# Attention scores on four 32-row tiles of TensorE, with the mask of the exponentials on GpSimd

## The chip, the core and the metric

The kernel runs on one core of a Trainium2 chip. The metric is the device time of one execution in microseconds (us); the median of three runs is compared. The names of the engines are those of the profile: PE is TensorE (its weight loads are PEld), DVE is VectorE, ACT is ScalarE, POOL is GpSimd, SP is the queue that issues DMA transfers.

## What is computed

The whole program is two layers of a transformer. The change touches one stage of it, the causal attention of layer 0, here called stage B:

```python
b, t, e = x.shape            # 8, 512, 128
k = (x @ Wk).reshape(b, t, h, s)     # h = 16 heads of s = 8
q = (x @ Wq).reshape(b, t, h, s)
v = (x @ Wv).reshape(b, t, h, s)
k = _layernorm(k, kln_w, kln_b)
q = _layernorm(q, qln_w, qln_b)
dot = jnp.einsum('bqhs,bkhs->bhqk', q, k) * scale
causal = jnp.tril(jnp.ones((t, t), dtype=bool))
dot = jnp.where(causal, dot, -jnp.inf)
attn = jax.nn.softmax(dot, axis=-1)
out = jnp.einsum('bhqk,bkhs->bqhs', attn, v).reshape(b, t, e)
return out @ Wo + bo
```

Everything is float32 to the outside; the scores are multiplied as float32r from numbers that are split into a high and a low part.

## The kernel before, in words

Stage A makes q, k and v of all tokens, stage C runs a mixture of experts, stage B is the attention, and stages D to G are the second layer. They follow each other in the order A, C, B, D and on. In stage B a head takes `SL = 32` columns: 8 for the values' high part, 8 and 8 for the split, 2 for the row's maximum. Four heads (`G = 4`) fill 128 columns and are a *group*. A batch has four groups (`NG`), and 8 batches make 32 groups.

For a group, PE transposes the four heads' keys (item K) and queries (item Q) through bank 6, and ACT copies them to SBUF. The scores are then computed twice. The first time they stand with queries on the partitions (units `q`, `scores_q`, L1739): eight units a group, unit i is query tile i // 2 and two of the four heads, and the score matmul of (qt + 1) x 128 columns is followed by a bf16 matmul of identity and mask (L1741) that adds -1e30 above the diagonal. DVE takes the row maxima of a unit (`max_q`, L951), and after eight units writes them, negated, into the queries' spare columns (`max_rows`, L958 and L959). PE transposes the queries again (item Z). The second time the scores stand with keys on the partitions (units `k`, `scores_k`, L1753), and the maximum is already subtracted. ACT takes the exponentials (`expo`, L1429), DVE puts zeros above the diagonal (`masked`, L967), and PE multiplies with the values (`weigh_values`, L1767), in four tiles of 32 columns of the array. Then come the transposes of the outputs (item O), DVE's division by the sums (`normalise`, L973 and L978), and once a batch the transposes A, the product with Wo (item W, L1797), and DVE's residual and statistics (`residual`, L987 to L998).

A score matmul contracts over 128 partitions although a head has only 32 of them. So the keys lie in `kp`, where each head has its own 128-row copy with zeros in the other heads' rows; four DMA transfers of SP a group (`spread_keys`, L533) put them there, and POOL clears `kp` once (L645). The units share three pairs of PSUM banks in turn (`pair_of_banks`, place in the stream of q and k units modulo 3), and `free_banks` makes PE wait until the unit three places before has been read.

The order of all of this is a table of numbers, `item_times`: each item has a time in units of which a group has 8, and every engine walks through the items in the order of these times. Items that fall before `AHEAD` belong to the round before: they are issued once ahead of the loop, and then in every pass of the loop for the next pass. A pass is two batches, so there are 4 passes:

```python
for time, item in times:
    if time < ahead:
        time += length
        self.early.add(item)
```

POOL is outside of that table. It normalises the keys and the queries of one batch after another (L668 to L681), pads the values (L687) and adds the output's bias (L694), and is held back by waits alone:

```python
for n, padded, ready in ((1, ks, B_ks), (0, qs, B_qs)):
    pool.wait_ge(B_mf, B_ROUNDS.passed("misc", hb, False, "KZ"[1 - n], g_last, 0))
```

## Time and profile before

| | before |
|---|---|
| median of 3 runs (lowest to highest) | 1348.21 us (1347.28 to 1350.85) |
| the profiled execution's own time | 1348.36 us |
| its span in the trace | 1346.3 us |
| PE busy | 1055.1 us (78%) |
| DVE busy | 871.3 us (65%) |
| ACT busy | 594.5 us (44%) |
| POOL busy | 417.8 us (31%) |
| mean granted clock of PE, of full speed | 0.907 |

Busy time is the time in which an engine had an instruction of its own under way. A matmul's row begins where it begins to stream and its end is modelled, so rows of matmuls overlap, and the start of the next one says more than the end of the last. An idle time in brackets stands with what ended it. The clock has two levels, 1.2 and 2.4 GHz; 1.00 is the upper one.

### The profile page before, as it was taken

The page shows a single profiled execution, that of the slowest core. Times are in us where ns is not written, and L with a number is a line of the kernel's source. Part 1 is how long each engine was busy: PE and PEld are TensorE (multiplying, and loading weights), DVE is VectorE, ACT ScalarE, POOL GpSimd, SP SyncE. Part 2 cuts the span into 40 slices and gives each one's busy share as a digit, 9 for nine tenths or more (in the row PEclk, how much of TensorE's full clock was granted, in tenths as well). Part 3 has the DMA queues.
Part 4 walks back from the last instruction along what each step waited for, and adds up shares of the span by engine and source line. Part 5 has one row for each costly group of instructions (what it writes and reads, how often), then busy time and mean ns, then how long its engine had stood idle before and what let it go on. Part 6 is the DMA issues. An engine that isn't in the chain of part 4 may idle for free.

```text
span 1346.3 us, 22600 instructions
## 1 busy us (share of the span) xinstructions
PE 1055.1 (78%) x6332; PEld 711.3 (53%) x6332; DVE 871.3 (65%) x1881; ACT 594.5 (44%) x1109; POOL 417.8 (31%) x460
## 2 busy tenths in 40 slices
PE   7699999879898989989898778877776321499970
PEld 4355544765555656656565454444444321399960
DVE  6677741247686777778677647999996555244445
ACT  6555554125464555555465555454454101144420
POOL 4100000771412124031000023355352177266660
PEclk9899999989998999999899989899998555699995
DMA  4011113321000000000000195000001011223206
GB/s 116 32 63 62 62 62 125 128 84 25 17 25 16 19 19 23 17 17 24 18 22 19 33 156 134 1 0 0 0 0 31 6 52 34 68 79 89 96 27 186
DMA packets 64911, 66.80 MB, mean 50 GB/s; under 512 B 7842, under 2 KB 53356, under 8 KB 62800
## 3 DMA queue, kind: packets, MB, share of 16 engines
q1 hardware_dynamic: 50256, 54.52, 14.9%
q0 software_dynamic: 4608, 6.61, 1.6%
q10 hardware_dynamic: 9984, 4.80, 1.3%
q8 instruction: 43, 0.70, 0.2%
q14 instruction: 20, 0.16, 0.0%
HBM read 29.90 MB, written 29.43 MB: 44 GB/s over the span
## 4 chain that ended last, share of the span: by engine, by line
PE 40%; DVE 17%; issue 12%; ACT 3%; POOL 2%; DMA 2%; DVEq 1%; POOLq 0%; ACTq 0%; SPq 0%
PE banks L1739 6%; PE banks L1753 6%; PE banks L1767 6%; PE banks L1799 5%; PE banks L2000 5%; PE banks L1992 4%; DVE D_gun L1123 2%; PE banks L1741 2%; DVE D_dmx L1079 2%; POOL rows_dram L776 2%; DVE B_mneg L951 1%; DVE D_sc L1110 1%; DMA F_back<-y_dram 1%; PE banks L1840 1%; ACT B_ot L1435 1%
## 5 line engine op out<-in xcount | busy, mean ns | idle before, releaser
L951 DVE TENSOR_REDUCE B_mneg<-banks 128x2 f32<-128x256 f32 (+3 forms) x273 | 223.9, 822 | 110.3 <-PE banks L1741 104.0
L1429 ACT ACTIVATE B_pt<-banks 128x1024 f32<-128x1024 f32 (+3 forms) x260 | 181.6, 708 | 146.2 <-PE banks L1753 144.8
L1739 PE MATMUL banks<-B_kp,B_qt 128*128 128x128 f32 (+3 forms) x546 | 181.4, 393 | 4.2 <-DMA B_kp<-B_kt 2.3
L1753 PE MATMUL banks<-B_qt,B_kp 128*128 128x512 f32 (+3 forms) x520 | 146.3, 363 | 13.3 <-issue 7.7
L1739 PEld LDWEIGHTS banks<-B_kp,B_qt 128*128 128x128 f32 x546 | 109.4, 201 | 62.9 <-ACT B_pt L1429 43.7
L1741 PE MATMUL banks<-B_mask_q,B_identb 128*128 128x128 bf16 x546 | 125.1, 234 | 0.0
L793 POOL DMA_INDIRECT y_dram<-F_yo,F_ide x80 | 80.7, 1009 | 67.0 <-DVE F_yo L1277 42.9
L1767 PE MATMUL banks<-B_pt,B_vp 128*32 128x512 f32 (+3 forms) x1024 | 98.3, 456 | 0.0
L1505 ACT ACTIVATE D_pr<-banks,D_dmx 128x512 f32<-128x512 f32 x69 | 47.5, 688 | 106.8 <-DVE D_dmx L1079 106.8
L1563 ACT ACTIVATE F_gh<-banks 128x512 f32<-128x512 f32 (+1 forms) x96 | 50.0, 527 | 100.5 <-PE banks L1992 96.1
L967 DVE SCALAR_TENSOR_TENSOR B_pt<-B_pt,B_mask_k 128x512 f32<-128x512 f32 x129 | 93.0, 721 | 1.6 <-DVE st L998 1.0
L1753 PEld LDWEIGHTS banks<-B_qt,B_kp 128*128 128x128 f32 x520 | 81.5, 197 | 15.5 <-issue 8.3
L776 POOL DMA_INDIRECT rows_dram<-F_xs,F_rowi x64 | 63.3, 988 | 58.3 <-issue 57.7
L1741 PEld LDWEIGHTS banks<-B_mask_q,B_identb 128*128 128x128 bf16 x546 | 53.6, 98 | 44.6 <-issue 19.4
L2000 PE MATMUL banks<-F_gw,F_gh 128*128 128x128 f32 x640 | 75.3, 275 | 0.0
L1882 PE MATMUL banks<-D_qk 128*128 128x512 f32 x138 | 74.7, 635 | 0.0
L2000 PEld LDWEIGHTS banks<-F_gw,F_gh 128*128 128x128 f32 x640 | 73.9, 192 | 0.6
L1420 ACT CAST B_qt<-banks 128x512 fp32r<-128x512 f32 x68 | 39.7, 584 | 59.9 <-PE banks L1799 59.9
L1379 ACT ACTIVATE C_ec<-banks,C_nmax 128x512 f32<-128x512 f32 x68 | 47.1, 699 | 38.5 <-DVE C_nmax L894 36.9
L633 POOL CAST B_identb<-ident 128x128 bf16<-128x128 f32 x1 | 0.3, 292 | 202.2 <-ACT C_eo L1402 202.2
L1079 DVE TENSOR_REDUCE D_dmx<-banks 128x1 f32<-128x512 f32 x69 | 47.2, 684 | 13.9 <-PE banks L1882 11.9
L667 POOL MEMSET B_qs<- 128x128 f32 x8 | 1.7, 213 | 172.2 <-PE banks L1799 171.7
(275 smaller groups left out, 2240.7 us busy)
## 6 DMA issues: line engine op xcount, KB each, us to landing
B_kp<-B_kt SPq DMA_DIRECT2D x144, 64.0 KB, 2.0
comb_dram<-C_comb SPq DMA_DIRECT2D x8, 1024.0 KB, 3.8
C_cst<-comb_dram SPq DMA_DIRECT2D x8, 1024.0 KB, 4.8
rows_dram<-D_zeros SPq DMA_DIRECT2D x8, 645.0 KB, 17.1
F_xe<-rows_dram SPq DMA_DIRECT2D x8, 645.0 KB, 4.1
C_w<-w_in SPq DMA_DIRECT2D x16, 256.0 KB, 2.8
y_dram<-D_zeros SPq DMA_DIRECT2D x2, 2048.0 KB, 17.8
F_gw<-mw_in SPq DMA_DIRECT2D x16, 256.0 KB, 3.1
```

Source lines behind the costliest of these rows:

```text
L776: pool.indirect_dma_start(out=rows_dram[:, :], out_offset=bass.IndirectOffsetOnAxis(ap=rowi[:, q, k, t:t + 1], axis=0), in_=xs[:, q, k, t, ...
L793: pool.indirect_dma_start(out=y_dram[:, :], out_offset=bass.IndirectOffsetOnAxis(ap=ide[:, par, m:m + 1], axis=0), in_=yo[:, par, m, :], i ...
L951: v.tensor_reduce(mneg[:, g % 2, qt, 2 * hp:2 * hp + 2], banks2[pair_of_banks(item)][:, :, 0:(qt + 1) * P], X, ALU.max, negate=True).then_ ...
L967: v.scalar_tensor_tensor(out=w, in0=w, scalar=BIG, in1=mask_k[:].unsqueeze(1).broadcast_to([P, G, P]), op0=ALU.min, op1=ALU.mult).then_inc ...
L1079: v.tensor_reduce(dmx[:, n:n + 1], bank[2 + n % 4][:], X, ALU.max, negate=True).then_inc(D_mx, 1)
L1429: a.activation(pt[:, 2 * hp:2 * hp + 2, PT_AT[kt]:PT_AT[kt] + w], banks2[pair_of_banks(item)][:, :, 0:w], ACT.Exp).then_inc(B_ex, 1)
L1739: t_.matmul(dst, qt1[:, g % 2, qt * P:(qt + 1) * P], kp[:, g % NG, 2 * hp + h, 0:(qt + 1) * P], start=True, stop=False)
L1741: ins = t_.matmul(banks2[ring][:, h, qt * P:(qt + 1) * P], identb[:], mask_q[:], start=False, stop=True)
L1753: ins = t_.matmul(dst, kp[:, g % NG, 2 * hp + h, kt * P:(kt + 1) * P], qt2[:, g % 2, kt * P:T], start=True, stop=True)
L1767: ins = t_.matmul(bank[7][SL * r:SL * r + SL, kt * P:T], vp[:, g // NG, kt, SL * h:SL * h + SL], pt[:, r, PT_AT[kt]:PT_AT[kt] + T - kt * P ...
L1882: t_.matmul(bank[2 + n % 4][:], qk[:, b, h, t * P:(t + 1) * P], qk[:, b, 2 + h, :], start=True, stop=True).then_inc(D_sf, 1)
L2000: ins = t_.matmul(bank[4 + alt][:, t * D:(t + 1) * D], gh[:, alt, m, t * P:(t + 1) * P], gw2[:, e, m, :], start=(m == 0), stop=(m == NJ - 1))
```

## The change

- **Scores.** `kp` is gone, with its DMA transfers and its clearing. A head's score matmul reads the head's 32 rows of `kt_` and of the queries, so it runs on one of four 32-row tiles of the array, in both layouts. The units of one query (or key) tile, which hold the four heads, now stand directly behind each other in the order, and the four mask matmuls of the q layout follow behind the four score matmuls. DVE is told of the first two heads after their two masks, and of the other two after theirs.
- **Mask of the exponentials.** It leaves DVE for POOL, as an `affine_select` of 128 x 512.
- **POOL's order.** POOL now walks through the same table: the five steps of each normalisation (`nk`, `nq`), the values (`nv`) and the bias (`nb`) have times, and stand between masks. Its wait for the end of stage C (`C_os`), which stood ahead of the first bias, now stands ahead of everything in the stage.
- **Last round.** The last pass stands behind the loop, without the early items of a round that does not follow: the loop has 3 passes.

Two stretches of the instruction order show it. The first is PE in the middle of the loop, at the step in which the q units of 128 columns stand. Before, this was the second half of one q unit (the couple of L1739 and L1741 stands twice in each), and what follows:

```order
L1739 MATMUL banks<-B_kp,B_qt 128x128
L1741 MATMUL banks<-B_mask_q,B_identb 128x128
L1753 MATMUL banks<-B_qt,B_kp 128x256 x2
L1759 REGISTER_ALU
L1767 MATMUL banks<-B_pt,B_vp 32x512 x4
L1726 REGISTER_ALU
```

After, the same place of PE's order:

```order
L1746 MATMUL banks<-B_kt,B_qt 128x128 x2
L1734 REGISTER_ALU
L1746 MATMUL banks<-B_kt,B_qt 128x128 x2
L1752 MATMUL banks<-B_mask_q,B_identb 128x128 x4
L1770 REGISTER_ALU
L1778 MATMUL banks<-B_pt,B_vp 32x512 x4
L1734 REGISTER_ALU
L1764 MATMUL banks<-B_qt,B_kt 128x256 x4
L1788 REGISTER_ALU
L1810 MATMUL banks<-ident,B_qs 128x128 x4
```

One q unit, one k unit and so on alternated; now a *quarter* of a group is four score matmuls, four masks, the four products with the values, four matmuls of the other layout and four transposes. L1734 is the register that a bank wait uses, and there is one between the two halves.

The second stretch is POOL at the head of the stage. Before, the wait for the end of stage C stood behind the values of the first batch:

```order
L681 TENSOR_TENSOR B_qs<-B_n,B_qs 128x64x8 [waits pool_own]
L684 ISA [waits B_q_split]
L687 ISA [waits B_pv]
L687 COPY B_vp<-qkv 128x16x8
```

```order
L694 ISA [waits C_out_sbuf]
L694 TENSOR_TENSOR x<-x,bo 128x512
```

After, it stands ahead of the first step of the keys:

```order
L639 TENSOR_SCALAR B_lnb<-B_ln 128x128 [waits pool_own]
L668 TENSOR_TENSOR B_n<-qkv,rst 128x512 [waits C_out_sbuf,pool_own,B_constants,B_misc_full]
L672 TENSOR_TENSOR B_n<-B_n,B_lnw 128x512 [waits pool_own]
L672 TENSOR_TENSOR B_n<-B_n,B_lnb 128x512 [waits pool_own]
L680 CAST B_ks<-B_n 128x128x8 [waits pool_own]
L683 TENSOR_TENSOR B_ks<-B_n,B_ks 128x64x8 [waits pool_own]
```

The normalisation of the first batch, ten steps, moved from before that wait to behind it.

```diff
-AHEAD = 16.2
+AHEAD = 16.5
 PG = 2 * NG
 
 
 def item_times():
     for g in range(PG):
         for i in range(8):
-            yield 8 * g + i, ("q", g, i)
-            yield 8 * g + i + 12.3, ("k", g, i)
+            yield 8 * g + 2 * (i // 2) + 0.01 * (i % 2), ("q", g, i)
+            yield 8 * g + 2 * (i // 2) + 13.1 + 0.01 * (i % 2), ("k", g, i)
         for kt in range(NT):
-            yield 8 * g + 2 * kt + 14.9, ("m", g, kt)
-            yield 8 * g + 2 * kt + 16.3, ("pv", g, kt)
+            yield 8 * g + 2 * kt + 14.95, ("m", g, kt)
+            yield 8 * g + 2 * kt + 16.9, ("pv", g, kt)
         yield 8 * g - 11.2, ("K", g, 0)
         yield 8 * g - 4.8, ("Q", g, 0)
         yield 8 * g + 9.6, ("Z", g, 0)
-        yield 8 * g + 22.4 + 16.3 - 15.5, ("O", g, 0)
+        yield 8 * g + 23.9, ("O", g, 0)
         if g % NG == NG - 1:
-            yield 8 * g + 24.0, ("A", g, 0)
+            yield 8 * g + 25.0, ("A", g, 0)
             yield 8 * g + 28.0, ("W", g, 0)
+    for b in range(PG // NG):
+        for n in range(5):
+            yield 8 * NG * b - 29.3 + 1.6 * n, ("nk", b, n)
+            yield 8 * NG * b - 21.3 + 1.6 * n, ("nq", b, n)
+        yield 8 * NG * b - 13.1, ("nv", b, 0)
+        yield 8 * NG * b - 11.1, ("nb", b, 0)
...
-        kp = Bm("kp", [P, NG, G, T], F32R)
-        kt_ = Bm("kt", [P, 2, T], F32R)
+        kt_ = Bm("kt", [P, NG, T], F32R)
...
-                    for r in range(G):
-                        rows = slice(SL * r, SL * r + SL)
-                        sp.dma_start(kp[rows, g % NG, r, :].bitcast(F32), kt_[rows, g % 2, :].bitcast(F32)
-                                     ).then_inc(B_kp[g % NG], 16)
...
-            g.memset(kp[:].bitcast(F32), 0.0).then_inc(B_const, 1)
...
+            pool.wait_ge(C_os, TILES + 4)
+
+            def pool_round(it, first, last=False):
+                skips = Skip(B_ROUNDS, pool, B_md, "m") if first else None
+
+                def masked(item):
+
+                    _, g_, kt = item
+                    pool.wait_ge(B_ex, B_ROUNDS.passed("k", it, item in EARLY, "k", g_, 2 * kt + 1))
+                    pool.sem_inc(turns, 1)
+                    w = pt[:, :, PT_AT[kt]:PT_AT[kt] + P]
+                    g.affine_select(out=w, in_=w, compare_op=ALU.is_ge, fill=0.0, base=0, pattern=[[0, G], [1, P]],
+                                    channel_multiplier=-1).then_inc(B_md, 1)
...
+                for item in B_ROUNDS.order:
+                    kind, b, n = item
+                    ahead = item in EARLY
+                    if kind not in ("m", "nk", "nq", "nv", "nb") or (first and not ahead) or (last and ahead):
+                        continue
+                    if kind == "m":
+                        masked(item)
+                        if first:
+                            skips.after(item)
+                    elif kind == "nk":
+                        normed(item, 1, ks, B_ks)
+                    elif kind == "nq":
+                        normed(item, 0, qs, B_qs)
...
-                    pool.wait_ge(C_os, TILES + 4)
-                    g.tensor_tensor(xb, xb, bo[:].unsqueeze(1).broadcast_to([P, NT, D]), ALU.add).then_inc(B_bo, 1)
...
+            pool_round(-1, True)
+            with pool.Fori(0, B // 2 - 1) as it:
+                own.loop(it, 2 * 2 * 4)
+                pool_round(it, False)
+            own.end_loop(B // 2 - 1)
+            pool_round(B // 2 - 1, False, True)
...
-                def masked(item):
-
-                    _, g, kt = item
-                    dve.wait_ge(B_ex, B_ROUNDS.passed("k", it, item in EARLY, "k", g, 2 * kt + 1))
-                    w = pt[:, :, PT_AT[kt]:PT_AT[kt] + P]
-                    v.scalar_tensor_tensor(out=w, in0=w, scalar=BIG, in1=mask_k[:].unsqueeze(1).broadcast_to([P, G, P]),
-                                           op0=ALU.min, op1=ALU.mult).then_inc(B_md, 1)
...
-                        act.wait_ge(B_kp[(g - 2) % NG], 64 * B_ROUNDS.passed(f"K{(g - 2) % NG}", it, item in EARLY, "K", g - 2, 0))
+                        act.wait_ge(B_s2, B_ROUNDS.passed("k", it, item in EARLY, "k", g - NG, 7))
...
-                        pe.wait_ge(B_kp[g % NG], 64 * B_ROUNDS.passed(f"K{g % NG}", it, item in EARLY, "K", g, 0))
                     for h in range(2):
-                        dst = banks2[ring][:, h, 0:(qt + 1) * P]
-                        t_.matmul(dst, qt1[:, g % 2, qt * P:(qt + 1) * P], kp[:, g % NG, 2 * hp + h, 0:(qt + 1) * P],
-                                  start=True, stop=False)
-                        ins = t_.matmul(banks2[ring][:, h, qt * P:(qt + 1) * P], identb[:], mask_q[:],
-                                        start=False, stop=True)
-                    ins.then_inc(B_s1, 1)
+                        rows = slice(SL * (2 * hp + h), SL * (2 * hp + h) + SL)
+                        t_.matmul(banks2[ring][:, h, 0:(qt + 1) * P], qt1[rows, g % 2, qt * P:(qt + 1) * P],
+                                  kt_[rows, g % NG, 0:(qt + 1) * P], start=True, stop=False)
+                    if hp == 0:
+                        return
+                    for pair in (pair_of_banks(("q", g, i - 1)), ring):
+                        for h in range(2):
+                            ins = t_.matmul(banks2[pair][:, h, qt * P:(qt + 1) * P], identb[:], mask_q[:],
+                                            start=False, stop=True)
+                        ins.then_inc(B_s1, 1)
...
-                        dst = banks2[ring][:, h, 0:T - kt * P]
-                        ins = t_.matmul(dst, kp[:, g % NG, 2 * hp + h, kt * P:(kt + 1) * P], qt2[:, g % 2, kt * P:T],
-                                        start=True, stop=True)
+                        rows = slice(SL * (2 * hp + h), SL * (2 * hp + h) + SL)
+                        ins = t_.matmul(banks2[ring][:, h, 0:T - kt * P], kt_[rows, g % NG, kt * P:(kt + 1) * P],
+                                        qt2[rows, g % 2, kt * P:T], start=True, stop=True)
...
-            with pe.Fori(0, B // 2) as it:
+            with pe.Fori(0, B // 2 - 1) as it:
                 pe_round(it, False)
+            pe_round(B // 2 - 1, False, True)
```

## Rows read from the trace of the kernel before

Windows: the stretch and its length, busy time (and instructions) of PE, PEld, DVE, ACT and POOL, granted clock, DMA share, GB/s. Timelines: start, length, engine, line, what, count, and in brackets the idle time before it and what ended it. Forms: line and what, count | busy us, mean ns | idle before.

**Rows 1.** Windows: three groups, a plain one of them, the last of the stage.
```profile
306.83:345.23 38.40, 36.85 (x290) 23.62 (x289) 30.33 (x50) 22.48 (x36) 7.97 (x7) 1.00 0.09 22
...
332.74:345.23 12.49, 12.26 (x98) 7.87 (x97) 9.97 (x17) 7.56 (x13) 6.70 (x6) 1.00 0.09 22
...
750.98:767.00 16.02, 13.85 (x107) 8.99 (x106) 10.74 (x20) 8.45 (x14) 0.00 (x0) 1.00 0.07 17
```

**Rows 2.** Timeline of PE: values, q units, a k unit, transposes.
```profile
479.64 1.07 PE L1767 MATMUL banks<-B_pt,B_vp 128*32 128x512 f32 x8
480.64 0.33 PE L1739 MATMUL banks<-B_kp,B_qt 128*128 128x128 f32 x1
...
481.03 0.48 PE L1753 MATMUL banks<-B_qt,B_kp 128*128 128x256 f32 x2
481.35 0.60 PE L1799 MATMUL banks<-ident,B_qs 128*128 128x128 f32 x4
...
492.27 0.43 PE L1767 MATMUL banks<-B_pt,B_vp 128*32 128x128 f32 x8
492.63 0.50 PE L1739 MATMUL banks<-B_kp,B_qt 128*128 128x512 f32 x1
492.97 0.23 PE L1741 MATMUL banks<-B_mask_q,B_identb 128*128 128x128 bf16 x1
493.01 0.48 PE L1739 MATMUL banks<-B_kp,B_qt 128*128 128x512 f32 x1
```

**Rows 3.** Timeline of PE's weight loads: column tiles, then whole arrays.
```profile
738.49 0.16 PEld L1767 LDWEIGHTS banks<-B_pt,B_vp 128*32 128x32 f32 x8
...
739.84 0.31 PEld L1753 LDWEIGHTS banks<-B_qt,B_kp 128*128 128x128 f32 x2
```

**Rows 4.** Forms on DVE, 300 to 760 us.
```profile
L967 DVE SCALAR_TENSOR_TENSOR B_pt<-B_pt,B_mask_k 128x512 f32<-128x512 f32 x128 | 92.4, 722 | 1.6 <-DVE st L998 1.0 <-ACT B_pt L1429 0.5
L951 DVE TENSOR_REDUCE B_mneg<-banks 128x2 f32<-128x1024 f32 x64 | 78.1, 1221 | 6.8 <-PE banks L1741 6.3
L951 DVE TENSOR_REDUCE B_mneg<-banks 128x2 f32<-128x768 f32 x66 | 63.2, 957 | 34.3 <-PE banks L1741 33.8
L951 DVE TENSOR_REDUCE B_mneg<-banks 128x2 f32<-128x512 f32 x64 | 44.2, 691 | 36.1 <-PE banks L1741 36.1
L951 DVE TENSOR_REDUCE B_mneg<-banks 128x2 f32<-128x256 f32 x64 | 27.1, 424 | 22.1 <-PE banks L1741 16.8 <-DVE B_atok L978 5.3
```

**Rows 5.** Forms on ACT, the same stretch: the longest exponentials.
```profile
L1429 ACT ACTIVATE B_pt<-banks 128x1024 f32<-128x1024 f32 x66 | 67.7, 1026 | 42.3 <-PE banks L1753 42.1 <-ACTq L124 0.2
```

**Rows 6.** Forms on POOL, whole span: a normalisation step, a small select.
```profile
L671 POOL TENSOR_TENSOR B_n<-B_n,B_lnw 128x512 f32<-128x512 f32 x16 | 22.4, 1399 | 1.3
...
L638 POOL TENSOR_SCALAR_AFFINE_SELECT B_mask_k<-B_mask_k 128x128 f32<-128x128 f32 x1 | 0.3, 293 | 0.1
```

**Rows 7.** Timelines of POOL and of DVE near 307 us.
```profile
306.82 1.28 POOL L681 TENSOR_TENSOR B_ks<-B_n,B_ks 128x512 fp32r<-128x512 f32 x1
...
307.01 1.13 DVE L958 CAST B_qs<-B_mneg 128x16 fp32r<-128x16 f32 x1
308.17 0.19 DVE L959 TENSOR_TENSOR B_qs<-B_mneg,B_qs 128x16 fp32r<-128x16 f32 x1
```

**Rows 8.** Timeline of PE where a batch ends.
```profile
359.73 0.66 PE L1799 MATMUL banks<-ident,B_atok 128*128 128x128 f32 x4 [2.56 <-DVEq L981]
...
361.05 1.94 PE L1767 MATMUL banks<-B_pt,B_vp 128*32 128x512 f32 x8
```

**Rows 9.** Timelines of POOL and PE at the head of the stage.
```profile
265.91 1.07 POOL L668 TENSOR_TENSOR B_n<-qkv,rst 128x512 f32 x1 [0.57 <-POOL B_lnb L652]
...
277.70 1.28 POOL L681 TENSOR_TENSOR B_qs<-B_n,B_qs 128x512 fp32r<-128x512 f32 x1
...
286.68 0.45 PE L1739 MATMUL banks<-B_kp,B_qt 128*128 128x128 f32 x1 [2.29 <-DMA B_kp<-B_kt]
```

**Rows 10.** Timeline of DVE: the last addition of stage C.
```profile
281.10 0.35 DVE L940 SCALAR_TENSOR_TENSOR x<-banks,C_crs,x 128x128 f32 x1 [0.54 <-PE banks L1711]
```

More of the change, by code:

```diff
@@ L23 @@
 NEG = -1.0e30
-BIG = 3.0e38
 PT_AT = (0, T, 2 * T - P, 3 * T - 3 * P)
@@ L1001, in dve_round @@
                     kind, g, i = item
-                    if first and item not in EARLY:
+                    if (first and item not in EARLY) or (last and item in EARLY):
                         continue
@@ L1438, in act_round @@
                     kind, g, i = item
-                    if first and item not in EARLY:
+                    if (first and item not in EARLY) or (last and item in EARLY):
                         continue
@@ L1722, in free_banks @@
                 def free_banks(item):
-                    before, earlier = B_ROUNDS.place_before("unit", item, 3, first)
+                    before, earlier = B_ROUNDS.place_before("unit", item, 3, first, last)
                     if before:
@@ L1803, in pe_round @@
                     kind, g, i = item
-                    if first and item not in EARLY:
+                    if (first and item not in EARLY) or (last and item in EARLY):
                         continue
-                    if kind == "m":
+                    if kind in ("m", "nk", "nq", "nv", "nb"):
                         continue
```

135 lines of the change are left out of this document (61 added, 74 removed).

## The prediction

> **What bounds the kernel now.** I read the busy times by windows first, then the timeline of PE, then the forms on the other engines. In a plain group of stage B PE is busy for 12.26 of 12.49 us, DVE for 9.97, ACT for 7.56 and POOL for 6.70 [rows 1]: what ends a group is PE's own work. The windows are cut where a group's first product with the values begins. From the first (306.83) to the last (750.98) there are 31 groups in 444.2 us; at 12.49 each they would take 387.2, so 57 us lie in the seven places where a batch ends. One of them shows what they are [rows 8]: the transposes A wait 2.56 us for DVE, and right behind that the values block takes 1.94 us where it took 1.07 elsewhere [rows 2]; PE was idle, and the block ran at the lower clock. So three things can be won: PE's work per group, the ends of batches, and the early items in the last pass.
>
> **PE's work per group.** I price blocks by the distance between starts. Four tiles side by side are in the trace already, by columns: the values block takes 1.00 us at 512 columns and 0.36 at 128 [rows 2], which is 0.15 fixed and 0.21 for each 128 columns. A score matmul is cheaper per column: in a row with its mask (0.04 us, 492.97 to 493.01) it takes 0.38 at 512, and two with their masks take 0.39 at 128 [rows 2], so 0.34 and 0.155 alone, or 0.06 for each 128 columns more. Four row tiles side by side are then 0.15 + 0.06 n, or 0.21, 0.27, 0.33, 0.39 us for n = 1 to 4. That is the cheap end. The dear end is no overlap: four scores in a row, 0.62, 0.87, 1.11, 1.36. Between them, with matmuls side by side and weight loads in a row, three loads at 0.12 (two take 0.31, one some 0.19) come on top: 0.57, 0.63, 0.69, 0.75. Eight loads of the column tiles take 0.16 us together [rows 3], 0.007 apart, so loads of different tiles do overlap; those are of 32 columns, ours of 128. I take 0.25, 0.30, 0.36, 0.41, near the cheap end. Four masks in a row: 0.04 each if their loads are covered and 0.10 each if not, and the array changes its form before and behind them; I take 0.30 a block. Four transposes take 0.43 with the change (they stand as 0.60 long, 0.17 of which is the tail) [rows 2].
>
> The changes of form can be seen only as part of the fixed 0.15 of the values block. The Trainium skill says (TensorEngine Tiling (Array Packing), Key Properties) that switching the tiling mode drains TensorE. A quarter now has five changes where it had two to three, so the trace's fixed part agrees with that, and by the rule alone nothing could be won at the 128-column forms.
>
> A quarter of a group on PE is then q block + masks + values (1.00, 0.78, 0.57, 0.36) + k block (256, 128, 512, 384 columns) + transposes: 2.3, 2.1, 2.1, 1.9, in all 8.3 us against 12.3. (Four k matmuls of 256 columns cost 0.64 now [rows 2], 0.30 then.)
>
> **But PE is no longer the bound.** The banks are three pairs, taken in turn. In the new order a quarter uses four units: q-a, q-b, k-a, k-b. By the modulo, q-a waits until DVE has read the q-b before it, and DVE cannot start until both q units and their first two masks are through. So PE and DVE take turns in a quarter: 0.05 us for the signal, the q block, 0.06 for the second mask, 0.26 for the last matmul's way and the signal, and two reductions. The reductions are 0.424, 0.691, 0.957 and 1.221 us [rows 4]. With the blocks above: 0.62 + 0.85 = 1.47; 0.67 + 1.38 = 2.05; 0.73 + 1.91 = 2.64; 0.78 + 2.44 = 3.22. The mask that leaves DVE (0.722 us, four a group [rows 4]) gives DVE 2.9 us a group, which this turn-taking uses up.
>
> In the first quarter DVE also has the row maxima and `normalise`, 1.3 us with their waits. These read SBUF, and POOL is in their way: the cast that takes 0.2 us elsewhere took 1.13 beside a POOL instruction that ended at 308.10, and its neighbour behind it 0.19 [rows 7]. POOL's work per group grows from 3.9 us (15.7 for a batch, ten steps like the 1.4 us of [rows 6] among it) by four masks. A select of 128 columns took 0.29 us; for 512 that is at most four times as much, 1.17, and 0.6 if most of the 0.29 is fixed. So POOL is busy for 60 to 80% of a group, and I add 1.0 us for the four short instructions. First quarter: 2.3 + 0.85 = 3.1, above PE's 2.3. Second: PE, 2.1. Third: 2.64 and 0.1 for a bank that waits on the exponentials (1.03 us each [rows 5]). Fourth: 3.22 + 0.2 for the same. Sum **11.35 us** for 12.49. Cheap end, without POOL in the way and with the cheap blocks: 10.3. Dear end, loads in a row: 3.15 + 2.8 + 3.0 + 3.6 = 12.55, and up to 13.
>
> The Trainium skill says (SBUF — State Buffer, The single rule) that VectorE and GpSimd share one pair of ports by an exclusive lock. Row and rule agree for the casts; by the rule the reductions, which read PSUM, stay untouched.
>
> The masks themselves hide. The longest case is the 512-column k block of the third quarter: its exponentials end about 4.0 us after that quarter's start, its mask 5.4 us (0.2 for the signals), and the values ask for it behind two quarters and a q block, 2.75 + 3.4 + 0.65 = 6.8 us. The cover is 1.4 us, which is one normalisation step that POOL may be in when the mask comes due; beyond it each us late is a us of PE. The transfers into `kp` are costed at nothing: SP has nothing else to issue, and only the first of them ended a wait [rows 9].
>
> **The sum, against the profiled execution's 1348.36 us** (span 1346.3; the median, 1348.21, is the same):
> - 29 plain steps (31 less two in the tail) x (12.49 - 11.35) = -33. Cheap end -64, dear end +15.
> - Ends of batches, 57 us: A stood 0.8 places behind O and stands 1.1 behind now, with a values block of 1.0 us between, so most of 2.56 us and of the lower clock behind it go; W's residual and statistics on DVE come on top where DVE now bounds. 57 becomes 42: -15, ends -25 and 0.
> - The last pass: its early q and k items go. In the last 16.02 us PE worked for 13.85 [rows 1], and in the group before as much. Two groups (12.5 + 16.0) become one chain of exponentials (six quarters' worth, some 7.6 us and two copies) and the same end: -12, ends -14 and -8.
> - The head: POOL's ten steps took from 265.91 to 278.98 [rows 9], ahead of stage C's end at 281.45 [rows 10]. They start there now: 281.65 + 13.1 = 294.8, the transposes at the lower clock 1.2, the copy 0.7: the first scores at 296.8 instead of 286.68. +10, ends +9 and +11. The transfers that ended the wait there (2.29 us [rows 9]) and the clearing of `kp` go, but neither is last any more.
>
> In all -50: **1298 us**.
>
> **The rivals.**
> - *The row tiles do not run side by side* (the other side). Blocks of 0.62 to 1.36 lengthen each turn: quarters of 3.15, 3.0, 3.5, 4.2, a group of 13.8, +39, with the other terms (-15, -8, +10) about 1374. For it: no row of this trace has 32-row tiles. Against: the column tiles overlap [rows 2, 3]. It decides from a group of 13.1 us, blocks some 0.43 us longer on average than mine.
> - *The turn-taking costs all of PE's gain*: POOL in the way more often, loads half in a row, a group of 12.5. What is left is -15 - 12 + 10: 1331.
> - *The lower clock.* PE idles 1 to 1.5 us in the last quarters. One idle time of 2.56 us brought the lower clock [rows 8]; if every second group falls to it for a quarter (+1.5 us), +22: 1320.
> - *Late masks.* A select over 2.4 us makes POOL the bound, 3.9 + 4 x 2.4 = 13.5 us a group, +29: 1360. The 0.29 us row speaks against it.
> - *Better than that*: cheap blocks, POOL seldom in the way, a group of 10.3: 1262 to 1267.
>
> **How the numbers follow.** My forecast 0.50 (1275 to 1320), the better case 0.12, the turn-taking 0.14, the clock 0.08, no overlap 0.12, late masks 0.04. The range leaves out part of the better case and the two slow ones: 1258 to 1352. About 0.3% (4 us) is what a measurement of this kernel tells from no change. Faster: 0.50 + 0.12 + 0.13 + 0.07 = 0.82; same 0.04; slower 0.14.
>
> **What would show it.** The distance of a group's first values blocks: 11.35 us, with DVE the last to end a wait of q units and PE idle for 2 to 3 us a group. Four scores of 512 columns less than 0.5 us from first start to the first mask. The select on POOL between 0.6 and 1.2 us, and L958 and L959 over 0.5 us on average. The first score near 297 us. No wait over 1 us ahead of A. The forecast is wrong if a group takes over 12.5 or under 10.3 us; if the four scores start 0.12 us or more apart it was the loads.

## The result, and the profile after

| | before | changed |
|---|---|---|
| median of four runs (lowest to highest) | 1349.53 us (1347.28 to 1353.77) | 1397.47 us (1390.08 to 1400.99) |
| ratio, 95% interval | | 1.034 [1.029, 1.039] |
| span of the profiled execution | 1346.3 us | 1399.1 us |
| start of the first group's values block | 306.83 | 323.40 |
| from there to the last group's: 31 steps | 444.2 us | 481.6 us |
| behind that block | 595.3 us | 594.1 us |

The kernel is 3.4% slower. Of the 52.8 us that its span grew by, 16.6 lie ahead of the first values block and 37.4 in the 31 steps behind it, which I call the **stage time** from here on. The page of the changed kernel, busy times and granted clock by slices:

```profile
PE 1078.8 (77%) x6224; PEld 655.8 (47%) x6224; DVE 762.6 (55%) x1731; ACT 580.4 (41%) x1097; POOL 483.1 (35%) x585
...
PEclk9899999966687768655858879999999655599995
```

Stage B fills the ninth to the twenty-fourth digit, and they are 5 to 8 where before they were 8 or 9, twelve of the sixteen 9. By windows (columns as in [rows 1]): the stage, a group with a high clock, one with a low.

```profile
323.40:805.03 481.63, 431.90 (x3002) 210.93 (x3001) 228.43 (x430) 229.58 (x373) 165.15 (x226) 0.72 0.00 1
416.41:428.63 12.22, 10.95 (x98) 5.57 (x97) 7.26 (x13) 7.34 (x12) 7.39 (x10) 0.95 0.01 1
607.43:624.44 17.01, 15.57 (x98) 7.46 (x97) 7.14 (x13) 7.45 (x12) 7.03 (x9) 0.60 0.00 1
```

The two groups hold the same work, and DVE and ACT are as busy in both. PE's 98 matmuls take 10.95 us in one and 15.57 in the other. The mean clock of the stage was 0.97 before and is 0.72 now. Cut finer, around the second of these groups, it is one of the two levels:

```profile
602.00:604.00 2.00, 1.22 (x16) 0.67 (x16) 0.46 (x1) 1.65 (x2) 0.19 (x1) 1.00 0.00 0
606.00:608.00 2.00, 2.00 (x15) 0.98 (x17) 1.45 (x6) 0.36 (x1) 1.48 (x2) 0.50 0.00 0
610.00:612.00 2.00, 2.00 (x16) 1.25 (x19) 0.20 (x1) 1.56 (x3) 0.75 (x2) 0.50 0.00 0
616.00:618.00 2.00, 2.00 (x17) 0.86 (x17) 1.68 (x2) 0.59 (x1) 0.56 (x1) 0.50 0.00 0
618.00:620.00 2.00, 1.04 (x8) 0.51 (x8) 0.00 (x0) 1.25 (x2) 0.00 (x0) 0.88 0.00 0
622.00:624.00 2.00, 2.00 (x12) 1.22 (x13) 1.66 (x5) 1.18 (x2) 0.94 (x2) 0.50 0.00 0
```

From 606 to 618 us it is at 1.2 GHz, although PE is busy all of the time; it comes back in a stretch in which PE is busy for 1.04 of 2.00 us, and is lost again at 622. The timeline of PE in the group at the high clock shows whether the blocks were priced rightly:

```profile
416.41 1.07 PE L1778 MATMUL banks<-B_pt,B_vp 128*32 128x512 f32 x8
417.40 0.39 PE L1764 MATMUL banks<-B_qt,B_kt 32*128 32x256 f32 x4
417.72 0.66 PE L1810 MATMUL banks<-ident,B_qs 128*128 128x128 f32 x4
418.31 0.63 PE L1746 MATMUL banks<-B_kt,B_qt 32*128 32x256 f32 x4
418.87 0.40 PE L1752 MATMUL banks<-B_mask_q,B_identb 128*128 128x128 bf16 x4
419.20 0.85 PE L1778 MATMUL banks<-B_pt,B_vp 128*32 128x384 f32 x8
...
420.83 0.45 PE L1746 MATMUL banks<-B_kt,B_qt 32*128 32x384 f32 x4
421.21 0.40 PE L1752 MATMUL banks<-B_mask_q,B_identb 128*128 128x128 bf16 x4
421.57 0.66 PE L1810 MATMUL banks<-ident,B_ks 128*128 128x128 f32 x4
422.16 0.64 PE L1778 MATMUL banks<-B_pt,B_vp 128*32 128x256 f32 x8
...
424.43 0.50 PE L1746 MATMUL banks<-B_kt,B_qt 32*128 32x512 f32 x2 [0.53 <-ACT B_pt L1436]
...
425.19 0.42 PE L1778 MATMUL banks<-B_pt,B_vp 128*32 128x128 f32 x8
...
426.47 0.44 PE L1764 MATMUL banks<-B_qt,B_kt 32*128 32x384 f32 x2 [0.48 <-DVE B_mneg L969]
...
428.63 1.08 PE L1778 MATMUL banks<-B_pt,B_vp 128*32 128x512 f32 x4
```

Four scores of 384 columns take 0.38 us to the masks and four of 256 take 0.32 us to the next block: the row tiles do run side by side. (Of the experiments below, the profiled executions of e4, e9, e10 and e14 took 24 to 43 us longer than the mean of the executions that their ratios are made from, which leave such slow ones out, so their stage times are too long by up to as much.) The other forms that the forecast spoke of (stage B; then the head of the stage):

```profile
L977 DVE TENSOR_TENSOR B_qs<-B_mneg,B_qs 128x16 fp32r<-128x16 f32 x32 | 6.1, 189 | 1.1
L976 DVE CAST B_qs<-B_mneg 128x16 fp32r<-128x16 f32 x32 | 5.8, 183 | 1.1
...
L653 POOL TENSOR_SCALAR_AFFINE_SELECT B_pt<-B_pt 128x512 f32<-128x512 f32 x128 | 81.2, 634 | 328.0 <-ACT B_pt L1436 327.0 <-POOL B_n L672 1.0
...
L1746 PE MATMUL banks<-B_kt,B_qt 32*128 32x512 f32 x128 | 31.1, 533 | 22.6 <-ACT B_pt L1436 17.4 <-DVE B_mneg L969 4.9
...
L1810 PE MATMUL banks<-ident,B_atok 128*128 128x128 f32 x32 | 7.5, 378 | 0.7 <-DVEq L991 0.7
...
283.19 1.07 POOL L668 TENSOR_TENSOR B_n<-qkv,rst 128x512 f32<-128x512 f32 x1 [24.07 <-DVE x L958]
...
299.10 0.48 PE L1746 MATMUL banks<-B_kt,B_qt 32*128 32x128 f32 x4
```

### The profile page after: what moved, and what is told of

Same layout as the page of the kernel before. It is cut to its first block, busy times and chain, and to the rows that moved or that the text cites. A ratio compares the mean times of both kernels' runs of the same rounds, so it can differ in the third digit from the quotient of the medians.

```text
span 1399.1 us, 21938 instructions
## 1 busy us (share of the span) xinstructions
PE 1078.8 (77%) x6224; PEld 655.8 (47%) x6224; DVE 762.6 (55%) x1731; ACT 580.4 (41%) x1097; POOL 483.1 (35%) x585
## 4 chain that ended last, share of the span: by engine, by line
PE 41%; DVE 16%; issue 10%; ACT 4%; POOL 3%; DMA 2%; DVEq 1%; POOLq 1%; ACTq 0%; SPq 0%
PE banks L1778 8%; PE banks L1810 7%; PE banks L2012 5%; PE banks L1746 4%; PE banks L2004 4%; PE banks L1764 4%; PE banks L1752 3%; DVE B_mneg L969 3%; DVE D_gun L1130 2%; ACT B_pt L1436 2%; DVE D_dmx L1086 2%; POOL rows_dram L794 2%; DVE D_sc L1117 1%; PE banks L1852 1%; DMA F_back<-y_dram 1%
## 5 line engine op out<-in xcount | busy, mean ns | idle before, releaser
L969 DVE TENSOR_REDUCE B_mneg<-banks 128x2 f32<-128x256 f32 (+3 forms) x256 | 199.2, 820 | 237.5 <-PE banks L1752 235.8
L653 POOL TENSOR_SCALAR_AFFINE_SELECT B_pt<-B_pt 128x512 f32<-128x512 f32 x128 | 81.2, 634 | 328.0 <-ACT B_pt L1436 327.0
L1778 PE MATMUL banks<-B_pt,B_vp 128*32 128x512 f32 (+3 forms) x1024 | 134.3, 607 | 5.5 <-issue 4.0
L1746 PE MATMUL banks<-B_kt,B_qt 32*128 32x384 f32 (+3 forms) x512 | 82.6, 509 | 27.7 <-ACT B_pt L1436 17.4
L1764 PE MATMUL banks<-B_qt,B_kt 32*128 32x256 f32 (+3 forms) x512 | 82.8, 495 | 18.7 <-DVE B_mneg L969 16.8
L1764 PEld LDWEIGHTS banks<-B_qt,B_kt 32*128 32x128 f32 x512 | 36.7, 220 | 126.0 <-issue 89.5
L1746 PEld LDWEIGHTS banks<-B_kt,B_qt 32*128 32x128 f32 x512 | 39.8, 240 | 72.5 <-ACT B_pt L1436 29.3
L1752 PE MATMUL banks<-B_mask_q,B_identb 128*128 128x128 bf16 x512 | 64.8, 266 | 0.0
L1810 PE MATMUL banks<-ident,B_qs 128*128 128x128 f32 x256 | 58.3, 369 | 6.5 <-POOL B_qs L683 5.5
L747 POOL TENSOR_TENSOR D_prod<-D_q 128x128 f32 (+7 forms) x32 | 44.0, 1406 | 21.7 <-POOLq L734 21.7
```

Of the source, the lines that this page charges most:

```text
L653: g.affine_select(out=w, in_=w, compare_op=ALU.is_ge, fill=0.0, base=0, pattern=[[0, G], [1, P]], channel_multiplier=-1).then_inc(B_md, 1)
L969: v.tensor_reduce(mneg[:, g % 2, qt, 2 * hp:2 * hp + 2], banks2[pair_of_banks(item)][:, :, 0:(qt + 1) * P], X, ALU.max, negate=True).then_ ...
L1746: t_.matmul(banks2[ring][:, h, 0:(qt + 1) * P], qt1[rows, g % 2, qt * P:(qt + 1) * P], kt_[rows, g % NG, 0:(qt + 1) * P], start=True, stop ...
L1752: ins = t_.matmul(banks2[pair][:, h, qt * P:(qt + 1) * P], identb[:], mask_q[:], start=False, stop=True)
L1764: ins = t_.matmul(banks2[ring][:, h, 0:T - kt * P], kt_[rows, g % NG, kt * P:(kt + 1) * P], qt2[rows, g % 2, kt * P:T], start=True, stop=True)
L1778: ins = t_.matmul(bank[7][SL * r:SL * r + SL, kt * P:T], vp[:, g // NG, kt, SL * h:SL * h + SL], pt[:, r, PT_AT[kt]:PT_AT[kt] + T - kt * P ...
```

## The experiments

Theory 1 is that the lower clock makes the loss, either by PE's new waits in the last quarter (1a) or because the scores run on 32 rows of the array, whatever PE's waits are (1b). The rivals: it is the new order and not the tiles; or the masks on GpSimd, or its late start, make the loss. The table has all runs. The stage times are the profiled executions'; *clock* is the mean of the stage. The rows marked * ran on chips on which the kernel before took 1414 to 1415 us, with nearly all of the difference behind stage B (655 us there in e13 against 596 in e7). So times are to be compared only within a row, with its ratio, and across rows by the stage time; the expectations of those rows, written in microseconds of the first chips, are read in the same way.

| kernel | median | ratio to before, 95% | stage time | clock |
|---|---|---|---|---|
| before | | 1 | 444.2 | 0.97 |
| changed | 1397.5 | 1.034 [1.029, 1.039] | 481.6 | 0.72 |
| e1 whole-array fillers | 1329.5 | 0.980 [0.976, 0.984] | 407.5 | 0.96 |
| e2 scores on the whole array | 1350.0 | 0.996 [0.992, 1.000] | 429.1 | 0.97 |
| e3 row tiles, old order | 1527.5 | 1.126 [1.121, 1.131] | 600.6 | 0.52 |
| e4 GpSimd early | 1380.1 | 1.015 [1.009, 1.021] | 494.9 | 0.69 |
| e6 fillers on 32 rows | 1383.7 | 1.020 [1.016, 1.024] | 465.1 | 0.79 |
| e7 = e1 + e4 | 1315.5 | 0.971 [0.968, 0.974] | 411.1 | 0.95 |
| e8 = e1, masks on DVE | 1355.9 | 1.000 [0.998, 1.003] | 439.6 | 0.91 |
| e9 = e3 + six fillers | 1619.3 | 1.193 [1.188, 1.198] | 735.8 | 0.50 |
| e10 = e9, fillers in rows * | 1649.4 | 1.147 [1.134, 1.160] | 681.7 | 0.54 |
| e11 = e1, fillers spread * | 1401.3 | 0.991 [0.988, 0.994] | 416.9 | 0.95 |
| e12 = e7, four fillers * | 1382.7 | 0.977 [0.972, 0.983] | 417.2 | 0.92 |
| e13 = e7, more at batch ends * | 1379.7 | 0.976 [0.970, 0.982] | 410.7 | 0.96 |
| e14 masks behind each pair * | 1488.7 | 1.045 [1.039, 1.052] | 523.7 | 0.66 |
| e15 q whole array, k tiles * | 1403.7 | 0.993 [0.990, 0.997] | 416.1 | 0.96 |
| e16 = e15 in the old order * | 1419.6 | 1.002 [1.000, 1.005] | 458.6 | 0.89 |

### The first four: clock, tiles, order, head

**e1** puts matmuls whose result nobody reads into the bank that the scores behind them overwrite, four ahead of the seventh q unit and two ahead of the third k unit of each group:

```diff
+                def fill(ring, n):
+                    for _ in range(n):
+                        t_.matmul(banks2[ring][:, 0, :], identb[:], fillb[:], start=True, stop=True)
...
+                    fill(ring, {6: 4}.get(i, 0))
...
+                    fill(ring, {2: 2}.get(i, 0))
```

> The changed kernel with six more bf16 matmuls of identity by a constant tile, 128 rows by 512 columns, per group: four into the bank of the third-turn unit q6 ahead of its scores, two into the bank of k2 ahead of its scores; all are overwritten by the scores, so they are work for nothing. They stand where TensorE waited for a bank in the changed kernel (0.5 us ahead of the last two score matmuls of 512 columns, 0.48 us ahead of the last two of 384). Theory 1, the lower clock is what costs, and it comes from the waits in the last quarter of a group: with the waits filled the granted clock of the stage is over 0.9, a group takes about 12.3 us instead of 17, and the whole 1320 to 1340 us. Theory 2, the turn-taking of TensorE and VectorE alone costs, the clock is a side effect: 1.3 us of added work a group, no gain, 1400 to 1435 us.

Windows of e1, a plain group, and the four fillers in its timeline:

```profile
360.62:372.48 11.86, 11.58 (x104) 5.65 (x102) 7.05 (x13) 7.36 (x12) 8.48 (x10) 1.00 0.01 2
...
367.63 1.04 PE L1742 MATMUL banks<-B_fillb,B_identb 128*128 128x512 bf16 x4 [0.17 <-DVE B_mneg L971]
```

With more work on PE the stage is 74 us shorter than the changed one's (407.5 against 481.6), and the kernel is 2.0% faster than before where the changed one was 3.4% slower. The time is what the first case expected, the clock of the stage is 0.96, and a plain group takes 11.86 us. The lower clock is the loss.

**e2** keeps the changed order and reads the keys from `kp` again, 128 rows, filled by DMA. The q part of the edit (the k part and the transfers are of the same kind):

```diff
-                        t_.matmul(banks2[ring][:, h, 0:(qt + 1) * P], qt1[rows, g % 2, qt * P:(qt + 1) * P],
-                                  kt_[rows, g % NG, 0:(qt + 1) * P], start=True, stop=False)
+                        t_.matmul(banks2[ring][:, h, 0:(qt + 1) * P], qt1[:, g % 2, qt * P:(qt + 1) * P],
+                                  kp[:, g % NG, 2 * hp + h, 0:(qt + 1) * P], start=True, stop=False)
...
```

> The changed kernel with its order of work, but the scores on the whole array again: 128-row matmuls from the spread keys kp, with the four transfers a group. One part of the change undone. Theory 1a, the clock falls because of the waits for banks: they are still there, so the stage stays at a mean clock of 0.7 to 0.8 and, with more matmul time per group, the whole takes 1430 to 1500 us. Theory 1b, the clock falls because matmuls of 32 rows (side by side) do not keep it up: the clock is over 0.93, a group takes 13.5 to 14 us, the whole 1370 to 1390 us.

**e3** is its counterpart: row tiles, but the alternating order of before, with each unit's two masks behind its two scores. The main part of the edit:

```diff
-            yield 8 * g + 2 * (i // 2) + 0.01 * (i % 2), ("q", g, i)
-            yield 8 * g + 2 * (i // 2) + 13.1 + 0.01 * (i % 2), ("k", g, i)
+            yield 8 * g + i, ("q", g, i)
+            yield 8 * g + i + 12.3, ("k", g, i)
...
```

> The changed kernel with its 32-row tiles, mask on GpSimd and shorter last pass, but the order of before: one q unit, one k unit, two masks behind the two scores of a unit. The other part of the change undone. Theory 1a (waits): TensorE has hardly a wait, the clock stays over 0.93, a group takes 10.5 to 11.5 us and the whole 1280 to 1320 us. Theory 1b (32-row matmuls): the clock falls as in the changed kernel, below 0.85, and the whole takes 1370 to 1430 us.

Windows of e3, a plain group and the one group in which the clock stayed up:

```profile
502.81:521.75 18.94, 18.94 (x99) 8.42 (x97) 7.42 (x12) 7.78 (x13) 2.54 (x4) 0.50 0.00 0
...
807.41:819.93 12.52, 11.39 (x99) 5.59 (x97) 8.71 (x21) 7.36 (x12) 4.09 (x8) 1.00 0.00 1
```

With the whole array the clock is 0.97 in the changed order; with row tiles it falls in both orders. So e2 clears the new order, and both kernels miss the times that case 1b gave them: e2's plain groups take 12.8 us (13.5 to 14 expected), and e3's 18.9, 1527 us in all (1370 to 1430 expected). In its one group at the upper clock e3 takes 12.52 us, no less than the 12.49 of before: row tiles in the old order would win nothing there even without the clock. In e3's plain group PE has no wait at all and the clock is 0.50: PE's waits can't be what keeps it down there, and 1a falls as the whole explanation. The Trainium skill (TensorE: Matmul & The Clock Gate, What's actually happening) says that the gate is set by how busy PE has been, and has no word on how many rows a matmul uses. By the profile's busy time e3 would then be at the upper level; the rows say the lower.

**e4** moves one wait of POOL back to where it stood:

```diff
-            pool.wait_ge(C_os, TILES + 4)
...
+                        if first:
+                            pool.wait_ge(C_os, TILES + 4)
                         xb = x[:, bass.ds((it + ahead) * (2 * NT) + b * NT, NT), :]
```

> The changed kernel with one edit: GpSimd's wait for the end of stage C stands ahead of the first bias again, not ahead of everything. The head term was put at 10 us, and the trace of the changed kernel shows the first score at 299.1 us against 286.7. All theories: 10 us less, 1385 to 1390 us; if something else at the head is late, under 4 us less.

The first values block starts at 310.26 instead of 323.40, 13.1 us earlier. By the ratios e4 is 1.9% under the changed kernel, about 26 us, but with intervals that also allow the 10 us expected (0.8 to 3.1%). What the clock did with the earlier start can't be read from its profiled execution; e7 gives the cleaner answer.

### What the fillers do

**e6** has the same fillers on 32 rows, `identb[0:SL, :], fillb[0:SL, :]`; **e7** adds e4 to e1; **e8** is e1 with the masks back on DVE, by the instruction of before (L967); **e9** puts fillers into e3, one each ahead of the first, third, fifth and seventh q unit and two ahead of the third k unit.

> The changed kernel with the same six extra matmuls a group, at the same two places and of the same 128x512 shape out, but on 32 rows of the array instead of 128. They fill the same idle time of PE. If the clock falls because PE has nothing to do in its waits, this is worth what the full-array fillers were: about 1330 us, clock 0.89, groups of 11.9 us. If only work on the whole array keeps it up, the clock stays near 0.8 or falls below it, and the fillers cost their own time at the lower clock: 1400 to 1450 us, groups of 17 to 18 us with PE busy all of it. Between the two (some 1360) it would be both.

> The full-array fillers and GpSimd's wait for the end of stage C put back ahead of its first bias, together. If the head is a fixed cost of its own, the first values block comes some 13 us earlier (near 311 instead of 324 us) and the time is 10 to 13 us under that with fillers alone: 1317 to 1321 us. If the earlier start is given back to the clock or to GpSimd's later work, it stays within 4 us of 1330.

> The full-array fillers, and the masks of the exponentials back on VectorE, four of 0.72 us a group; GpSimd keeps everything else. If VectorE and PE take turns as forecast, VectorE's 2.9 us a group lengthen the turns by 1 to 2.9 us: 30 x that is 30 to 87 us, 1360 to 1415 us. If VectorE waits for PE at those places anyway, the masks cost nothing: within 5 us of 1330. Under that, GpSimd's masks would have been late.

> The 32-row tiles in the alternating order of before, which ran at clock 0.72 with PE never idle, with six full-array fillers a group (0.2 us each at the upper clock). PE has no waits there to be filled, so if only busy time counted, they could only add: 1.2 us a group at the upper clock, 2.4 at the lower, 1560 to 1600 us. If it is the share of whole-array work that holds the clock, they bring it up: groups of 12.5 to 13.7 us and 1345 to 1385 us, the earlier 18.9 us groups gone. If six are too few, the clock rises for part of the stage and the time lies between.

Windows of e6, two groups that follow the same program:

```profile
484.59:496.45 11.86, 11.44 (x105) 5.93 (x103) 7.05 (x13) 7.36 (x12) 7.05 (x9) 1.00 0.00 0
...
602.60:619.57 16.97, 16.76 (x104) 8.04 (x103) 7.14 (x13) 7.43 (x12) 7.01 (x9) 0.60 0.00 1
```

The fillers of e6 fill the same waits, and win 17 us of stage time where whole-array ones win 74; the ratios tell the same (1.020 and 0.980 for 1.034). So filling the waits gives about a quarter of it, and the rest is that the work is on the whole array. e7 starts 13.7 us earlier than e1 and gives 3.5 back in the stage: the head is a cost of its own, 9 us net in the span and 1% by the two ratios, as expected.

e8 shows what the move to GpSimd is worth beside the fillers: without it the stage is 32 us longer, part of it by the clock (0.91 for 0.96). Its windows, and DVE's timeline in that group:

```profile
352.54:364.92 12.38, 11.62 (x103) 5.66 (x103) 10.64 (x17) 7.36 (x12) 6.76 (x6) 1.00 0.00 0
...
359.60 1.23 DVE L991 SCALAR_TENSOR_TENSOR B_pt<-B_pt,B_mask_k 128x512 f32<-128x512 f32 x1
361.46 2.36 DVE L975 TENSOR_REDUCE B_mneg<-banks 128x2 f32<-128x1024 f32 x2 [0.63 <-PE banks L1775]
```

A group is 0.4 to 1.6 us longer at the same clock, less than DVE's 3.6 us more of busy time, and the seven steps with a batch end are 2.3 us longer each (135.5 against 119.4), at a lower clock. So DVE and PE do take turns, for less than the 1 to 2.9 us a group that was expected, and the rival on GpSimd's masks is wrong: they are a gain.

e9 went against theory 1b as I had put it. Six fillers a group did not bring the clock up in the old order; they cost 4.3 us a group at the lower level (23.27 against 18.93), more than the 2.4 expected. That opened the question of the next kernels.

### Place, number and order

**e10** is e9 with the fillers where e1 has them; **e11** is e1 with those of e9; **e12** leaves the two ahead of the k unit out of e7; **e13** adds three to e7 behind each product with Wo.

> The 32-row tiles in the alternating order of before, with the same six full-array fillers a group, but at the places where they helped the changed order: four in a row and two in a row, instead of one at a time. One at a time they left the clock at its lower level for the whole stage (groups of 23.3 us). If it was their spreading, four in a row bring the clock up: groups of 12.9 to 13.7 us, 1350 to 1400 us. If the alternating order itself holds the clock down, groups stay at 23 us and the time near 1620.

> The changed order with six full-array fillers a group, four of them one at a time (ahead of the first q unit of each quarter), two ahead of the k units of the second quarter. Against the same six in bursts of four and two (1329.5 us). If only a burst holds the clock up, this falls back towards 1380 to 1400 us, clock near 0.82. If their number counts and not their place, 1325 to 1335 us, clock 0.89.

> With GpSimd started early, only the four fillers of the fourth quarter, without the two ahead of the second quarter's k units. If four are enough, the group is no longer than 11.86 us and the time is that of six or up to 5 us less: 1310 to 1316 us. If the clock needs all six, it falls in part of the stage: 1330 to 1365 us.

> With GpSimd started early and all six fillers, three more once a batch, behind the product with Wo. They cost 0.7 us each time, some 5 us in all. In five of seven places where a batch ends the clock still fell behind that product's waits, for 1 to 5 us each, some 13 us together. If whole-array work there keeps it up, a gain of 5 to 10 us: 1306 to 1311 us. If the clock falls by the idle time itself, nothing is won and the fillers cost 5 us: 1318 to 1322 us.

Windows of e10, neighbouring groups:

```profile
536.30:549.85 13.55, 13.10 (x104) 6.19 (x102) 7.46 (x13) 7.64 (x13) 2.54 (x4) 1.00 0.00 0
549.85:572.11 22.26, 22.26 (x105) 9.34 (x103) 7.68 (x13) 7.96 (x13) 7.04 (x8) 0.50 0.01 1
```

For the clock it makes little difference whether the fillers stand in rows or one at a time: in the old order both fail (0.50 one at a time; 0.54 in rows, where three of the 31 steps ran near the upper clock), in the changed order both work (0.96 and 0.95). Spread, they cost more: a plain group takes 12.13 instead of 11.86 us, and 23.27 instead of 22.25 in the old order. With four of them the clock still holds in plain groups but falls more often where a batch ends, 6 us in all. e13 holds it there a little better, and pays as much for its fillers as it wins.

**e14** takes the changed order and puts each pair's masks behind its own scores again; no matmul is added or removed:

```diff
-                    if hp == 0:
-                        return
-                    for pair in (pair_of_banks(("q", g, i - 1)), ring):
-                        for h in range(2):
-                            ins = t_.matmul(banks2[pair][:, h, qt * P:(qt + 1) * P], identb[:], mask_q[:],
-                                            start=False, stop=True)
-                        ins.then_inc(B_s1, 1)
+                    for h in range(2):
+                        ins = t_.matmul(banks2[ring][:, h, qt * P:(qt + 1) * P], identb[:], mask_q[:],
+                                        start=False, stop=True)
+                    ins.then_inc(B_s1, 1)
```

> The changed order, where each pair of q scores is followed by its own two masks again: two more changes a quarter between 32-row scores and whole-array masks, every matmul the same. VectorE hears of the first two heads earlier, so at the upper clock a group would be 0.3 to 0.8 us shorter. If it is the alternation of 32-row and whole-array work that brings the clock down, it falls towards the alternating order's 0.72: 1430 to 1520 us (against 1397). If only the amount of 32-row work counts, the clock stays near 0.81: 1375 to 1405 us.

**e15** takes only the q layout back to the whole array (the q part of e2's edit), and **e16** is the same in the old order.

> The changed order with the q layout on the whole array again (copies by DMA) and the k layout on 32-row tiles: half the 32-row work. Groups at the upper clock between 12.2 (both on tiles) and 12.8 us (neither). If the clock goes with the amount of 32-row work, it lies between 0.81 and 0.895: 1355 to 1385 us. If it needs both layouts on tiles, it is that of the whole array: clock 0.89 to 0.90, 1340 to 1352 us.

> The same half in the alternating order of before: q layout on the whole array, k layout on 32-row tiles, GpSimd's masks. If the alternating order is bad by the alternation of q scores and masks alone, this is cured here and the clock is near 0.9: 1340 to 1365 us. If 32-row work between whole-array work brings it down, it stays low: clock 0.75 to 0.82, 1400 to 1480 us.

A plain group of e14 by windows, and one of e15 with its longest q block:

```profile
488.62:507.25 18.63, 18.10 (x97) 8.06 (x96) 7.60 (x12) 7.43 (x12) 7.32 (x10) 0.50 0.00 0
```

```profile
475.24:487.47 12.23, 11.20 (x98) 6.39 (x96) 7.05 (x13) 7.34 (x12) 8.50 (x11) 1.00 0.09 23
...
482.51 1.56 PE L1773 MATMUL banks<-B_kp,B_qt 128*128 128x512 f32 x4 [0.35 <-DVE B_mneg L995]
483.91 0.40 PE L1779 MATMUL banks<-B_mask_q,B_identb 128*128 128x128 bf16 x4
```

In e14 only two masks a quarter change places and the clock goes from 0.72 to 0.66; by the ratios that is 1% of the time (1.045 against 1.034, some 15 us, with intervals that all but meet), by the stage times at most 42. Read as a ratio, 1.045 lies just above what the amount of 32-row work alone was to give (1375 to 1405 us, up to 1.04) and short of what the alternation was to give (1430 us, 1.06, and more). In e15 PE does more work a group than the changed kernel (1.40 us for four scores of 512 columns, 482.51 to 483.91, that take 0.47 on row tiles in e1), waits for nearly as long (1.03 us a group for 1.27, 0.35 and 0.48 of it for DVE), and the clock is 0.96. That is the cleanest run against the waits: with waits of the same kind the clock is up when half the scores use the whole array. Over the whole stage PE is idle for 51 us in e15 and for 50 in the changed kernel, at clocks of 0.96 and 0.72, and for 32 us in e1 and 30 in e6, at 0.96 and 0.79: the clock doesn't follow the idle time. The old order does no harm by itself either, as the kernel before shows (0.97): it is bad together with row tiles in both layouts (e3, 0.52), far less with the k layout's alone (e16, 0.89), which came out near the first case of its expectation (1.002 of before).

**What is settled**: the lower clock makes the loss; it comes with scores on 32-row tiles in both layouts, hardly with the k layout's alone (e15), and is much worse in the alternating order (e3). The masks between the pairs of scores (e14) are a small part of that at least. **What stays open**: whether it takes both layouts or the q layout's tiles alone would do it, since no run had only those; and why the same whole-array fillers that hold the clock up in the changed order do next to nothing in the old one. Their grouping doesn't tell, more than six a group were not tried there, and no run separated the alternation from two tiles being in use at a time instead of four.

**The best version** run is e7, at 0.971 [0.968, 0.974] of the time before: the changed kernel, the fillers, and POOL's wait where it was. The intervals of e12 and e13 overlap with its own.

## Why the prediction was wrong

The forecast was 1298 us, and 1397 lies outside the range. **The step that failed is the rival "the lower clock"**: its condition, its price and its chance. It made idle time the condition, took 1 to 1.5 us of it a group, and had every second group lose 1.5 us, 22 us in all, at a chance of 0.08. PE's waits in the group at the high clock are 1.27 us (12.22 less 10.95), as the rival had them, and it isn't mainly they that decide (e6, e15). Take the seven steps with a batch end and the last two apart: the other 22 average 14.75 us in the changed kernel and 12.20 in e1, where the clock is up nearly throughout. That is 2.5 us on every group and not 1.5 on every second; over the 31 steps it is 74 us for the 22 that the rival had. I read [rows 8], one wait and then one slow block, as a rule on waits; no row of the trace had row tiles, so none could show what they do to the clock, and I bounded their cost from the side of duration alone. The row on PE's busy share was in the way, too: it counts a 32-row matmul as it counts one of 128 rows.

Term by term:

- *Plain groups*: forecast -33 for 29 of them. The 22 steps took 293.1 us before and 324.5 after, +31; in e1 268.5, -25. Before, eight of the 22 still held part of a batch's end; the 14 that held none took 12.49 us before, 14.08 after and 11.88 in e1.
- *The group at the upper clock*: forecast 11.35 us; 12.22 at a clock of 0.95. The blocks of four scores were mostly right (0.32 and 0.38 us for a forecast 0.30 and 0.36, and nowhere the loads in a row), but the q block of 256 columns took 0.56 us to its masks (418.31 to 418.87) for 0.30. PE's own work was not right: 10.95 us where I summed 8.3. From values block to values block the four quarters took 2.79, 2.96, 3.03 and 3.44 us, for 3.1, 2.1, 2.75 and 3.4. The second is the one that is off most: it has two blocks of transposes, of queries and of keys, where I had given each quarter one (the third has none); each takes 0.59 us (421.57 to 422.16), not 0.43, and the masks in front of a values block or of the keys' transposes 0.33 and 0.36 where I had 0.30.
- *The turn-taking* is real, as e8 shows and as the waits for ACT's and DVE's reads (0.53 and 0.48 us) do. But the longest wait for the banks of q units ends with ACT's exponentials, 17.4 us over the stage ahead of the scores of 512 columns against 4.9 for DVE (L1746), where I had DVE last. The Trainium skill (TensorEngine Tiling (Array Packing), PSUM Bottleneck) says that tiling speeds up TensorE and not the reading of PSUM; by these two waits the trace agrees.
- *POOL in DVE's way*: forecast +1.0 us a group from L958 and L959 (now L976 and L977) at over 0.5 us. They take 0.18 and 0.19: POOL's long steps now stand in the order between its masks, and in no group of the stage was L976 beside a POOL instruction, nor was L977 lengthened by one (0.19 us at most). In e8 one DVE mask took 1.23 us beside a POOL cast that ended at 360.29, where it took 0.72 on average before, so the wait exists where they meet.
- *The select on POOL*: forecast 0.6 to 1.17, with 0.6 if most of the small one's 0.29 us is fixed; 0.634. No mask was late to speak of: PE waited 1.5 us for them in the whole stage.
- *Batch ends and last pass*: forecast -15 and -12. The seven steps with a batch end and the last two took 151.0 us before, 157.1 after and 139.0 in e1. Over plain groups of their own length (12.49 and 11.86), the 29 steps ahead of the last two hold 57 us before and 44 in e1: -13, so the first term was right, and in the changed kernel the clock hides it. The wait ahead of A is gone, 0.7 us for all eight blocks of it where one was 2.56. The last two steps and what lies behind them came out 5.6 us shorter (6.1 in e1), about half of what the second term had.
- *The head*: forecast first scores at 296.8, +10. They came at 299.10, +12.4: POOL's first step began at 283.19 where I had put 281.65, and a block of key transposes of 1.27 us that I had left out stood ahead of the scores. The way from there to the first values block grew by 4.2 us, at clock 0.50 where it had been 0.86.

Without the lower clock the prediction would have been right in its direction, with about twice the gain that there is: e1, with its fillers in waits that are there anyway, ran at 0.980 of before, or 1323 us, for my 1298, just outside 1275 to 1320 and inside the full range. By the spans of the profiled executions e1 is 20 us under the kernel before where the forecast had 50; of the 30 between, 15 are the underpriced group, 29 x (11.86 - 11.35), 7 the head, 6 the last pass and 2 the batch ends.

## What to carry to other kernels

Small contractions packed into row tiles finish sooner at the same clock (four scores of 512 columns 0.47 us for 1.40), and can still lose by the clock. Before and after such a change compare the granted clock of the stage, not PE's busy share: here a stage in which PE was hardly ever idle ran at 1.2 GHz (e3). If it falls, put part of the tiled work back on the whole array (e15, q layout), group the tiled matmuls instead of alternating them (0.72 against 0.52 here, which was not enough), or add a few whole-array matmuls in the waits (e1, which did nothing in the alternating order), and measure which is enough.

## What the runs showed of the hardware that was not expected

- PE at the lower clock with no idle time over whole groups: 18.94 busy us of 18.94, clock 0.50, with 32-row scores in two layouts (e3).
- More matmuls, less time: six whole-array ones a group took the stage from 481.6 to 407.5 us (e1). The same six with 32 rows gave 465.1 (e6).
- The same program holds both states: in e6 the same kind of group takes 11.86 us at clock 1.00 and 16.97 at 0.60, each at least twice in a row.
- A select of 512 columns takes GpSimd 0.634 us where one of 128 took 0.293 [rows 6].
